# Expert stage with the weights stationary, token blocks of 448 rows and pad rows written beforehand

## The chip, the cores and the metric

The kernel runs on one core of one Trainium2 chip. Its time is the device time of one execution, in microseconds (us). The kernel before took 530.7 us, the median of three runs (530.37 to 531.23).

## The reference, cut to what matters

Cross attention and then a mixture of experts, in float32, on 16 sequences of 100 tokens with 256 features (1,600 tokens).

```python
x = x + xattn(layernorm(x), ctx, ctx, ...)   # 16 heads of 16, rope, window of the last 65 keys
h = layernorm(x)                             # 1600 x 256
probs = softmax(h @ router_w.T)              # 8 experts
topk_p, topk_i = top_k(probs, 2); topk_p /= topk_p.sum(-1)
for e in range(8):
    mask = (topk_i == e).any(-1)
    mean_w = w_tok.sum() / max(mask.sum(), 1)      # w_tok: the weights of e, one number per expert results
    eo = (silu(h @ gate_w[e].T) * (h @ up_w[e].T)) @ down_w[e].T    # 256 -> 1024 -> 256
    out += mask[:, None] * eo * mean_w
x = x + out
```

A token needs only its two chosen experts: 3,200 rows of work over eight experts.

## The kernel before

Attention stage (0 to about 200 us). The sequences go in eight pairs, in software pipeline. Loops over pair i and slot n (0 to 7) are written out in line, and each engine (`@block.tensor`, `scalar`, `vector`, `gpsimd`, `sync`) has its own order of work in them; semaphores are the only link. SyncE (SP) loads context and x in three parts (`load_rows`, L343): pair 0, pair 1, and, behind the key copies of pair 0, all the rest (L372). `key_blocks` (L354) copies the rotated keys of a pair into a block layout by 16 small transfers. ScalarE (ACT) loads the weights of expert 0 in slot 1 of pair 1 (L742). VectorE (DVE) asks for the third part of x in slot 7 of pair 0 (`xn_stats(2)`, L1037, L862), before the first maximum of pair 1. GpSimd (POOL) splits the weights of expert 0 and scatters each pair's normalized rows, with the row's number behind its 256 features, to the DRAM table `slots`, which has one region per expert (`scatter`, L1181).

Hand-over. DVE counts the tokens of each expert and makes from them the plan: the first and last tile of each expert, in one word that every engine loads (`tiles_of`, L241). POOL fills the rows behind each expert's last token with a pad row that points to spare output rows (L1222, eight indirect writes); SP waits for these and for the scatters before it loads tiles (L384 to L394).

Expert stage. A step is a tile of 128 rows of one expert. Matmuls run on float32r values that are split into a rounded high part and a remainder, and three products (high x high, high x low, low x high) make one. The token tile, transposed to features by tokens, is the stationary operand, and 512 weight columns move (`hidden`, L620; `three_products`, L611); this gives tokens by hidden features, which are transposed back in 128 x 128 pieces (`hidden_transpose`, L628) for the down projection (`project_down`, L635). ACT applies silu and rounds the high parts, DVE multiplies gate and up and takes the remainders. POOL scales the output by the expert's mean weight and adds it to `out` by an accumulating indirect write (L1245, L1250). The weights of expert e+1 are split on ACT and DVE during the first three steps of expert e, in twelve pieces of 512 columns, from one of two raw buffers. A loop over four pairs of experts holds two loops over tiles; the routing of these inputs gives 30 steps.

## Time and profile before

| | before |
|---|---|
| median of the runs | 530.7 us |
| fastest run | 530.37 us |
| span of the profiled execution | 528.9 us |
| TensorE busy | 476.4 us, 90% |
| VectorE, ScalarE, GpSimd busy | 321.5, 265.6, 186.4 us |
| attention stage, hand-over | 0 to 200 us, 200 to 224.7 us |
| expert stage, first to last matmul | 224.7 to 516.1 us |
| data moved | 46.26 MB |

The span is that of one profiled execution, from its first to its last instruction; for that execution no other time is given, and it is set beside the runs' median. The page gives the busy time of each engine, the span in 40 slices (13.2 us each) and the costliest groups of instructions. In the span's order, TensorE is nearly full in the attention stage, nearly empty in the hand-over and full again in the expert stage. In a row, the mean length of one matmul is longer than the distance between two, since matmuls overlap in the array; the distance is read from the starts.

### The profile page before, as it was taken

The numbers are of one execution on the slowest core, as the hardware profiler recorded it, in microseconds if no ns is written. First come the engines' busy times: TensorE is split into PE (matmuls) and PEld (weight loads), VectorE is DVE, ScalarE is ACT, GpSimd is POOL, SyncE is SP. The second block draws the span as 40 slices with busy tenths as digits, with TensorE's granted clock in tenths as the row PEclk, the third lists the DMA queues.
The fourth block names the chain that finished last, engine by engine and source line by source line (L and its number), as shares of the span: only waits on it lengthen the run. The fifth ranks groups of instructions, "written<-read, shape, count | busy, mean of one in ns | idle before, by whom it ended". The sixth has DMA issues, their size and how long they took to land. (4 is left out here: it accounts for less than half of the span.)

```text
span 528.9 us, 10721 instructions
## 1 busy us (share of the span) xinstructions
PE 476.4 (90%) x2879; PEld 375.3 (71%) x2880; DVE 321.5 (61%) x827; ACT 265.6 (50%) x878; POOL 186.4 (35%) x211
## 2 busy tenths in 40 slices
PE   2999999999999983199999999999999999999980
PEld 2656666665666542078888888888888888888870
DVE  3476988989998656345665456655655555553430
ACT  1287777677777870044544445544444444532320
POOL 5201327355372434712332323323333232232232
PEclk9699999999999995579999999999999999999996
DMA  7166102112020171371531634415317212112110
GB/s 210 33 184 241 32 12 54 32 34 63 7 58 14 50 286 47 96 274 32 168 117 35 215 83 139 147 32 196 101 20 256 42 20 32 27 21 39 20 20 10
DMA packets 21738, 46.26 MB, mean 87 GB/s; under 512 B 5032, under 2 KB 18600, under 8 KB 20684
## 3 DMA queue, kind: packets, MB, share of 16 engines
q10 hardware_dynamic: 1982, 23.29, 11.6%
q1 hardware_dynamic: 12974, 14.34, 9.3%
q0 software_dynamic: 6752, 8.29, 9.2%
q8 instruction: 11, 0.18, 0.1%
q14 instruction: 19, 0.16, 0.1%
HBM read 34.21 MB, written 10.04 MB: 84 GB/s over the span
## 5 line engine op out<-in xcount | busy, mean ns | idle before, releaser
L752 ACT ACTIVATE probs<-b_s,negmax 100x100 f32<-100x100 f32 x256 | 85.6, 358 | 25.2 <-DVE negmax L1005 21.8
L615 PE MATMUL b_s<-w_hi,x_hi 128*128 128x512 f32 x180 | 77.1, 428 | 1.1 <-issue 1.1
L617 PE MATMUL b_s<-w_hi,x_lo 128*128 128x512 f32 x180 | 72.3, 402 | 0.0
L616 PE MATMUL b_s<-w_lo,x_hi 128*128 128x512 f32 x180 | 72.2, 401 | 0.0
L640 PE MATMUL b_pv<-w_hi,h_hi 128*128 128x256 f32 x240 | 69.8, 291 | 1.4 <-DVE h_lo L1102 1.4
L640 PE MATMUL b_pv<-w_hi,h_lo 128*128 128x256 f32 x240 | 67.4, 281 | 0.0
L640 PE MATMUL b_pv<-w_lo,h_hi 128*128 128x256 f32 x240 | 67.3, 280 | 0.0
L1245 POOL TENSOR_SCALAR y_sb<-y_raw,mean 128x256 f32<-128x256 f32 x30 | 32.8, 1093 | 75.9 <-DVE y_raw L1109 75.7
L1250 POOL DMA_INDIRECT out<-y_sb,idnow x30 | 49.1, 1638 | 25.6 <-issue 23.0
L780 ACT CAST h_hi<-b_small 128x512 fp32r<-128x512 f32 x30 | 17.6, 587 | 80.7 <-PE b_small L631 80.7
L1116 DVE TENSOR_TENSOR w_lo<-w_raw,w_hi x84 | 57.3, 682 | 0.0
L752 ACT ACTIVATION_READ_ACCUMULATOR probs<-b_s,negmax 100x1 f32 x256 | 55.9, 218 | 0.0
L421 PE MATMUL b_s<-kblk,qrot 128*100 128x400 f32 x128 | 54.3, 505 | 0.0
L1102 DVE TENSOR_TENSOR h_lo<-b_small,h_hi 128x512 fp32r<-128x512 f32 x30 | 20.8, 692 | 55.0 <-ACT h_hi L780 55.0
L787 ACT CAST w_hi<-w_raw x84 | 52.2, 621 | 0.0
L776 ACT ACTIVATE act<-b_s 128x512 f32<-128x512 f32 x60 | 36.0, 600 | 28.6 <-PE b_s L617 28.6
L640 PEld LDWEIGHTS b_pv<-w_hi,h_hi 128*128 128x128 f32 x240 | 45.2, 188 | 3.0 <-DVE h_lo L1102 1.6
L640 PEld LDWEIGHTS b_pv<-w_lo,h_hi 128*128 128x128 f32 x240 | 45.3, 189 | 1.4
L640 PEld LDWEIGHTS b_pv<-w_hi,h_lo 128*128 128x128 f32 x240 | 45.2, 188 | 0.0
L1005 DVE TENSOR_REDUCE negmax<-b_s 100x4 f32<-100x400 f32 x64 | 36.2, 565 | 14.8 <-PE b_s L421 14.2
L1097 DVE TENSOR_TENSOR h_sb<-b_s,act 128x512 f32<-128x512 f32 x30 | 20.8, 692 | 34.7 <-PE b_s L617 34.7
L1176 POOL TENSOR_SCALAR ve<-mv 100x2 f32<-100x2 f32 x16 | 3.6, 228 | 103.8 <-DVE mv L859 103.8
(142 smaller groups left out, 1004.1 us busy)
## 6 DMA issues: line engine op xcount, KB each, us to landing
w_raw<-in_ffw ACTq DMA_DIRECT2D x7, 3072.0 KB, 10.1
xin<-slots SPq DMA_DIRECT2D x30, 128.5 KB
w_raw<-in_ffw SPq DMA_DIRECT2D x1, 3072.0 KB, 10.8
kblk<-krot SPq DMA_DIRECT2D x128, 12.5 KB, 1.8
out<-x_all SPq DMA_DIRECT2D x8, 200.0 KB
ctx_all<-in_ctxT SPq DMA_DIRECT2D x1, 1200.0 KB, 6.1
x_all<-in_x SPq DMA_DIRECT2D x1, 1200.0 KB
cst<-in_consts SPq DMA_DIRECT2D x1, 539.0 KB, 7.5
```

Of the source, the lines that this page charges most:

```text
L421: pe.matmul(o, qrot[:, i % 2, 2 * c + b, :], kblk[:, i % 2, c, h:h + QH, b * S:(b + 1) * S], start=False, stop=True).then_inc(s_s, 1)
L615: pe.matmul(o, lh, rh, start=(k == 0), stop=False)
L616: pe.matmul(o, lh, rl, start=False, stop=False)
L617: m = pe.matmul(o, ll, rh, start=False, stop=(k == n - 1))
L640: m = pe.matmul(b_y[:, 0:D], left[:, f, :], right[:, f, :], start=(f == 0 and k == 0), stop=(f == FC - 1 and k == 2))
L752: m = nc.scalar.activation(probs[:, N % 3, h, :], b_s[N % 3][0:S, h * S:(h + 1) * S], ACT.Exp, bias=negmax[:, N % 4, h:h + 1], accum_out=p ...
L776: nc.scalar.activation(act[:, half, :], b_gate[half][:, :], ACT.Silu).then_inc(s_act, 1)
L787: nc.scalar.copy(w_hi[1 - par][:, bass.ds(col, WC)], w_raw[par][:, bass.ds(col, WC)]).then_inc(s_whi, 1)
L1005: V.tensor_reduce(negmax[:, N % 4, :], b_s[N % 3][0:S, 0:QH * S].rearrange("p (h s) -> p h s", h=QH), AX.X, ALU.max, negate=True).then_inc ...
L1116: V.tensor_tensor(w_lo[1 - par][:, bass.ds(col, WC)], w_raw[par][:, bass.ds(col, WC)], w_hi[1 - par][:, bass.ds(col, WC)], ALU.subtract).t ...
L1245: G.tensor_scalar(y_sb[:, :], y_raw[:, :], mean1[:, 0:1], None, ALU.mult).then_inc(s_scaled, 1)
L1250: G.indirect_dma_start(out, bass.IndirectOffsetOnAxis(idnow[:, 0:1], 0), y_sb[:, :], None, bounds_check=TOK + P - 1, oob_is_err=True, comp ...
```

## The change

A block is now 448 rows of one expert: 4 groups of 112. A partition of the loaded block `xin` holds four successive rows of the table. The weights are the stationary operand, 128 hidden features at a time (chunk f, 0 to 7), and 448 tokens move; the result has hidden features on partitions and goes to the down projection without a transpose, where the hidden values are stationary and 256 weight columns move. Four row groups collect in two PSUM banks. ACT scales and evicts the output; POOL issues four accumulating writes per block. The experts are written out one after the other on each engine. The first block of an expert, in line, carries the splitting of the next expert's weights, in six pieces of 1,024 columns (half of a gate, up or down matrix), from one raw buffer that is refilled piece by piece; further blocks would run in a loop that the plan skips where an expert has one block.

The eight tail writes and the counts for them are gone. Instead ACT's queue writes pad rows over the whole table, in four transfers from a host array `padrows` in slot 1 of pairs 0, 2, 3 and 5, and each scatter waits for the parts that it can reach. The store of pad output rows covers 448 rows, comes from `padrows` and no longer waits for a memset. SP's register loads for expert 0 stand ahead of its wait for the scatters.

The diff, cut; conversions of x and of hidden values on ACT and DVE go by halves and chunks in the same way.

```diff
-TILE = 128
+GRP = 4
+ROWS = 112
+TILE = GRP * ROWS
 MAXT = -(-TOK // TILE)
-REGION = MAXT * TILE + TILE
+REGION = MAXT * TILE
...
-WC = 512
+WC = WT // 2
+WCH = 6
+FILLS = (0, 2, 3, 5)
...
+    pads = np.zeros((TILE, RW), np.float32)
+    pads[:, D:] = (TOK + np.arange(TILE, dtype=np.int32))[:, None].view(np.float32)
...
-            sp.wait_ge(s_zero, 2)
-            sp.dma_start(out[TOK:TOK + P, :], tailrow[:, 0:D]).then_inc(s_pad, 16)
+            sp.dma_start(out[TOK:TOK + TILE, :], padrows[:, 0:D]).then_inc(s_pad, 16)
...
-            sp.dma_start(w_raw[0][:, :], ffw[1]).then_inc(s_raw[0], 16)
+            for k in range(WCH):
+                sp.dma_start(w_raw[:, k * WC:(k + 1) * WC], ffw[1][:, k * WC:(k + 1) * WC]).then_inc(s_raw[k], 16)
...
-                sp.wait_ge(s_tails[e], 16)
+                if e == 0:
+                    for q in s_scat:
+                        sp.wait_ge(q, 16 * TOPK * 2 * (NPAIR // 2))
...
-                    sp.dma_start(xin[:, :], slots[bass.ds(row, TILE), :]).then_inc(s_in, 16)
+                    sp.dma_start(xin[:, :, :].rearrange("p g w -> p (g w)"),
+                                 slots[bass.ds(row, TILE), :].rearrange("(p g) w -> p (g w)", g=GRP)
+                                 ).then_inc(s_in, 16)
...
+            def hidden(par, t, f):
+                cols = slice(f * P, (f + 1) * P)
+                for which, banks, done in ((0, b_gate, s_gate), (1, b_up, s_up)):
+                    wh, wl = wpart(w_hi[par])[which], wpart(w_lo[par])[which]
+                    o = banks[f % 2][:, 0:TILE]
+                    for c in range(DC):
+                        if f == 0 and which == 0:
+                            pe.wait_ge(s_xlo, DC * t + c + 1)
+                        pe.matmul(o, wh[:, c, cols], x_hi[:, c, :], start=(c == 0), stop=False)
+                        pe.matmul(o, wh[:, c, cols], x_lo[:, c, :], start=False, stop=False)
+                        m = pe.matmul(o, wl[:, c, cols], x_hi[:, c, :], start=False, stop=(c == DC - 1))
+                    m.then_inc(done, 1)
+            def project_down(par, t, f):
+                pe.wait_ge(s_hlo, FC * t + f + 1)
+                if f == 0:
+                    pe.wait_ge(s_y, t + 1)
...
+                for g in range(GRP):
+                    o = b_y[g // 2][0:ROWS, g % 2 * D:(g % 2 + 1) * D]
+                    for k, (left, right) in enumerate(((h_hi, wh), (h_hi, wl), (h_lo, wh))):
+                        m = pe.matmul(o, left[:, f, g * ROWS:(g + 1) * ROWS], right[:, f, :],
...
+            def step(t, par, next_par, next_split, last):
+                for f in range(1, FC):
+                    if f >= 2:
+                        pe.wait_ge(s_h, FC * t + f - 1)
+                    if f == FC - 1 and not last:
+                        pe.wait_ge(s_xlo, DC * t + DC)
+                        tile_transpose(t + 1)
+                    hidden(par, t, f)
+                    if f >= 2:
+                        project_down(par, t, f - 2)
+                project_down(par, t, FC - 2)
+                if not last:
+                    pe.wait_ge(s_wlo, next_split)
+                    hidden(next_par, t + 1, 0)
+                project_down(par, t, FC - 1)
...
+            for e in range(E):
+                par = e % 2
+                lo, hi, end = tiles_of(pe, e)
+                with pe.If(end - lo), pe.Fori(lo, end) as t:
+                    step(t, par, par, WCH * (e + 1), False)
+                step(end, par, 1 - par, WCH * (e + 2), e == E - 1)
...
+            def fill_pads(j):
+                a.dma_start(slots.rearrange("(e j p g) w -> j e p (g w)", j=MAXT, p=ROWS, g=GRP)[j],
+                            padrows.rearrange("(p g) w -> p (g w)", g=GRP).unsqueeze(0)
+                            .to_broadcast([E, ROWS, GRP * RW])).then_inc(s_pre[j], 16)
...
+                    if n == 1 and i in FILLS:
+                        fill_pads(FILLS.index(i))
...
+            def take_output(t, e):
+                a.wait_ge(s_down, t + 1)
+                a.wait_ge(s_idnow, t + 1)
+                a.wait_ge(s_mean, 1)
+                for n in range(GRP // 2):
+                    m = nc.scalar.activation(y_sb[:, 2 * n:2 * n + 2, :].rearrange("p g d -> p (g d)"),
+                                             b_y[n][0:ROWS, :], ACT.Copy, scale=meanw[0:ROWS, e:e + 1])
+                m.then_inc(s_y, 1)
+            def step(t, e, par, split, again, final=False):
+                for f in range(FC):
+                    if f:
+                        if f == FC - 1 and not final:
+                            a.wait_ge(s_up, FC * (t + 1))
+                            x_high(t + 1)
+                        silu(t, f)
+                    hidden_high(t, f)
+                    if split and f < WCH:
+                        weights_high(e, par, f)
+                    if split and again and 1 <= f <= WCH:
+                        reload(e, f - 1)
                 if not final:
                     silu(t + 1, 0)
+                take_output(t, e)
...
+                for j in range(MAXT):
+                    if j * TILE < (i + 1) * PT:
+                        g.wait_ge(s_pre[j], 16)
...
+                for n in range(GRP):
+                    G.indirect_dma_start(out, bass.IndirectOffsetOnAxis(idnow[:, n:n + 1], 0), y_sb[:, n, :], None,
```

## Rows read from the trace of the kernel before

**Rows 1.** The page: TensorE's share, and its clock in 40 slices.

```profile
PE 476.4 (90%) x2879; PEld 375.3 (71%) x2880; DVE 321.5 (61%) x827; ACT 265.6 (50%) x878; POOL 186.4 (35%) x211
...
PEclk9699999999999995579999999999999999999996
```

**Rows 2.** TensorE's waits, 230.9 to 516.1 us: total, times, longest.

```profile
PE b_pv L640 <- DVE h_lo L1102: 1.4, 1, 1.4
```

**Rows 3.** Stretches: PE, PEld, DVE, ACT, POOL busy us (count), clock, DMA share, GB/s.

```profile
224.70:230.70 6.00, 5.46 (x12) 3.82 (x12) 0.49 (x1) 1.24 (x2) 2.02 (x4) 0.50 0.50 132
230.90:516.10 285.20, 283.71 (x1726) 249.93 (x1726) 154.08 (x292) 124.83 (x232) 86.89 (x93) 1.00 0.33 92
```

**Rows 4.** TensorE in order of time: start, length, line, shape.

```profile
383.71 0.60 PE L631 MATMUL b_small<-cst,h_sb 128*128 128x128 f32 x4
384.07 0.48 PE L615 MATMUL b_s<-w_hi,x_hi 128*128 128x512 f32 x1
384.38 0.40 PE L616 MATMUL b_s<-w_lo,x_hi 128*128 128x512 f32 x1
...
386.73 0.39 PE L617 MATMUL b_pt<-w_hi,x_lo 128*128 128x512 f32 x1
...
387.30 0.28 PE L640 MATMUL b_pv<-w_lo,h_hi 128*128 128x256 f32 x1
...
388.47 0.28 PE L640 MATMUL b_pv<-w_hi,h_lo 128*128 128x256 f32 x1
```

**Rows 5.** Groups of conversions: count, busy us, mean ns.

```profile
L1116 DVE TENSOR_TENSOR w_lo<-w_raw,w_hi x84 | 57.3, 682 | 0.0
...
L787 ACT CAST w_hi<-w_raw x84 | 52.2, 621 | 0.0
```

**Rows 6.** SP's waits over the span.

```profile
SPq L385 <- DMA slots<-xrow,desti: 16.2, 1, 16.2
```

**Rows 7.** Order of time, 201 to 225 us, SP, POOL and TensorE.

```profile
201.43 0.29 SPq L367 DMA_DIRECT2D out<-x_all  x1
...
213.92 0.99 POOL L1186 DMA_INDIRECT slots<-xrow,desti  x1 [0.30 <-issue]
...
215.22 0.99 POOL L1186 DMA_INDIRECT slots<-xrow,desti  x1 [0.30 <-issue]
...
221.20 0.00 SPq L394 DMA_DIRECT2D xin<-slots  x1
...
222.91 0.66 PE L608 MATMUL b_proj<-cst,xin 128*128 128x128 f32 x2 [6.27 <-DMA xin<-slots]
...
224.71 0.77 PE L615 MATMUL b_s<-w_hi,x_hi 128*128 128x512 f32 x1 [1.14 <-issue]
```

**Rows 8.** Four stretches, columns as in rows 3.

```profile
28.00:36.00 8.00, 7.57 (x51) 4.58 (x50) 6.05 (x14) 7.04 (x36) 0.00 (x0) 1.00 0.75 201
36.00:38.00 2.00, 2.00 (x10) 1.42 (x9) 1.45 (x4) 1.84 (x10) 0.00 (x0) 1.00 0.23 58
38.00:40.00 2.00, 1.64 (x12) 0.82 (x10) 1.62 (x4) 1.27 (x7) 0.00 (x0) 1.00 0.08 20
46.00:50.00 4.00, 4.00 (x26) 3.20 (x25) 3.17 (x8) 3.14 (x14) 0.00 (x0) 1.00 1.00 430
```

**Rows 9.** DMA queues from 9 to 10 us: packets, MB, share.

```profile
q10 hardware_dynamic: 86, 0.21, 75.4%
q1 hardware_dynamic: 90, 0.07, 26.8%
```

**Rows 10.** SP's transfers in order of time, 20 to 64 us.

```profile
23.70 0.61 SPq L344 DMA_DIRECT2D ctx_all<-in_ctxT  x1
24.35 0.54 SPq L345 DMA_DIRECT2D x_all<-in_x  x1
```

**Rows 11.** DVE at the end of pair 0.

```profile
39.47 0.74 DVE L855 BATCH_NORM_STATS2 stats<-x_all 100x6 f32<-100x256 f32 x2
```

**Rows 12.** The last write of the kernel.

```profile
518.55 1.60 POOL L1250 DMA_INDIRECT out<-y_sb,idnow  x1 [0.84 <-issue]
```

More of the change, by code:

```diff
@@ L61 @@
 C_BASE = C_EXP + E
-C_TAIL = C_BASE + E
-C_THR = C_TAIL + E
+C_THR = C_BASE + E
 C_LT = C_THR + E * (MAXT - 1)
@@ L317, in build @@
         s_in = sem("s_in")
-        s_xt = sem("s_xt")
+        s_xt = [sem(f"s_xt{c}") for c in range(DC)]
         s_xhi = sem("s_xhi")
@@ L637, in project_down @@
+                    m.then_inc(done, 1)
[3 more added lines that the diff above has]
+                    pe.wait_ge(s_y, t + 1)
                 wh, wl = wpart(w_hi[par])[2], wpart(w_lo[par])[2]
-                for f in range(half * HF, (half + 1) * HF):
+                for g in range(GRP):
+                    o = b_y[g // 2][0:ROWS, g % 2 * D:(g % 2 + 1) * D]
                     for k, (left, right) in enumerate(((h_hi, wh), (h_hi, wl), (h_lo, wh))):
-                        m = pe.matmul(b_y[:, 0:D], left[:, f, :], right[:, f, :],
-                                      start=(f == 0 and k == 0), stop=(f == FC - 1 and k == 2))
@@ L783, in weights_high @@
[L783 to L800 removed]
+                for c in range(DC):
+                    a.wait_ge(s_xt[c], t + 1 + c)
+                    nc.scalar.copy(x_hi[:, c, :], b_xt[c][:, 0:TILE]).then_inc(s_xhi, 1)
@@ new lines, in step, with expert, last_expert @@
+                take_output(t, e)
+            def expert(e, par, again):
+                lo, hi, end = tiles_of(a, e)
+                step(lo, e, par, True, again)
+                with a.If(end - lo), a.Fori(lo + 1, hi) as t:
+                    step(t, e, par, False, False)
+            def last_expert(e, par):
+                lo, hi, end = tiles_of(a, e)
+                with a.If(end - lo), a.Fori(lo, end) as t:
+                    step(t, e, par, False, False)
+                step(end, e, par, False, False, final=True)
@@ L828, in _ @@
             x_high(0)
             silu(0, 0)
-            with a.Fori(0, E // 2 - 1) as ep:
-                for par in range(2):
-                    expert(2 * ep + par, par, a.to_reg(16 * (ep + 2 - par)), True)
-            expert(E - 2, 0, 16 * (E // 2 + 1), False)
-            expert(E - 1, 1, None, False)
+            for e in range(E - 1):
+                expert(e, e % 2, e + 2 < E)
+            last_expert(E - 1, 1)
         @block.vector
@@ L1091, in take_ids @@
+            def take_ids(t):
                 v.wait_ge(s_in, 16 * (t + 1))
[L1092 to L1103 removed]
@@ new lines, in step @@
+            def step(t, e, par, split, final=False):
+                for f in range(FC):
+                    if f:
+                        if f == FC - 1 and not final:
+                            x_low(t + 1)
+                        gated(t, f)
+                    hidden_low(t, f)
+                    if split and f < WCH:
+                        weights_low(e, par, f)
+                    if f == FC - 2 and not final:
+                        v.wait_ge(s_idnow, t + 1)
+                        take_ids(t + 1)
@@ L1134, in step, with expert @@
                 if not final:
                     gated(t + 1, 0)
[L1137 to L1152 removed]
+            def expert(e, par):
+                lo, hi, end = tiles_of(v, e)
+                step(lo, e, par, True)
+                with v.If(end - lo), v.Fori(lo + 1, hi) as t:
+                    step(t, e, par, False)
@@ L1154, in _, with last_expert @@
+            def last_expert(e, par):
+                lo, hi, end = tiles_of(v, e)
+                with v.If(end - lo), v.Fori(lo, end) as t:
+                    step(t, e, par, False)
+                step(end, e, par, False, final=True)
             x_low(0)
-            take_ids(0, slice(0, 1))
+            take_ids(0)
             gated(0, 0)
-            with v.Fori(0, E // 2 - 1) as ep:
-                for par in range(2):
-                    expert(2 * ep + par, par, True)
-            expert(E - 2, 0, True)
@@ L1161, in _ @@
-            expert(E - 1, 1, False)
+            for e in range(E - 1):
+                expert(e, e % 2)
+            last_expert(E - 1, 1)
         @block.gpsimd
```

342 lines of the change are left out of this document (90 added, 252 removed).

## The prediction

> **What bounds the kernel now.** I read the page's busy shares and clock row first, then the waits of the expert stage, then stretches of it, and last the order of single instructions. TensorE is busy 90% of the span; its granted clock falls to the lower level (1.2 GHz) twice, in the second slice (13 to 26 us) and from 200 us until the expert stage is under way [rows 1]. In the expert stage TensorE's longest wait in 285 us is 1.4 us [rows 2], and it is busy 283.7 of 285.2 us at the upper level [rows 3]. So that stage is worth what TensorE's instructions cost, and nothing else. The attention stage (0 to 200 us) is a fixed order on five engines with about 3 us of slack between neighbours; what enters it late is paid in full.
>
> How the pieces are priced [rows 4]: ten 512-column matmuls start in 2.35 us, 0.235 each; ten 256-column ones in 1.17 us, 0.117 each; four transposes take 0.36 us and delay the matmul behind them by 0.08, 0.11 each. A step of today is 24 x 0.235 + 24 x 0.117 + 10 x 0.11 = 9.55 us; 30 of them, less the 2.8 us of matmuls that the last one lacks, make 283.7 us, which is the busy time of [rows 3].
>
> **The change, part by part.**
>
> Number of blocks. Today's 30 steps are 128-row tiles. The inputs' routing gives the experts 374, 410, 299, 390, 438, 418, 425 and 446 tokens (the reference's top-2 choice, counted). All are under 448, so there are 8 blocks, one per expert, and no loop over blocks ever runs a second time.
>
> TensorE. Hidden: 8 blocks x 8 chunks x 2 (gate, up) x 2 x 3 = 768 matmuls of 448 columns, at 0.235 x 448/512 = 0.206: 157.9 us (today 720 x 0.235 = 169.2). Down: 8 x 8 x 4 row groups x 3 = 768 of 256 columns at 0.117: 89.9 us (today 84.2; it grows, since 112 of 128 output rows are used). Transposes of the hidden values (240) vanish, since the hidden values now come out with features on partitions; those of tokens are 8 a block, 56 behind the first, 6.9 us with the delays. The first 6 us run at the lower clock as today [rows 3]: 3.2 us more. Waits 0.5. Sum 258.4, against 516.1 - 224.7 = 291.4: **-33.0 us**. Nine tenths of it are the transposes; in columns the two kernels nearly tie. Bounds: a 448-column matmul from 0.187 (columns at the ideal share of 2.4 GHz) to 0.235, -47 to -10; I take the proportional value, because 256 and 512 columns are proportional within 1%.
>
> Does ACT and DVE work keep up? A chunk is 12 x 0.206 + 12 x 0.117 = 3.88 us of TensorE. A converted 512-column piece costs 0.62 on ACT and 0.68 on DVE [rows 5]. Per chunk a chain runs: product on DVE (at most 0.68), its rounding on ACT (0.62), weight piece of 1,024 columns on ACT (at most 1.24), its remainder on DVE (at most 1.36), then the next product: 3.9, with two hops of 0.1 at most 4.1, and 3.7 if fixed cost is shared. Six such chunks fall behind by at most 1.3 us; the hidden matmuls of chunk f need only the product of f-2, which leaves 1.4 us. So 0. If it is late the cost is (chain - 3.88) x 6 x 7: 0 to +15. The token conversion between blocks (after the last hidden matmul: 0.62 and 0.68 for the first half, plus hops, 1.5) lies under two down chunks (2.8). The output pass on ACT (1.2) lies under two hidden chunks (4.9). The six 512 KB reloads have a whole block (32 us) to land; today 3 MB needs a third of that. Queued behind ACT's output pass is the rounding of the next block's first chunk, needed 4.9 us later.
>
> Hand-over. Today SP waits 16.2 us from the end of its last store issue (201.7) for the scatters, to 217.9, then issues the first token load at 221.2 [rows 6, 7]; it has landed at 222.9, and the first hidden matmul starts at 224.7 [rows 7]. The eight tail writes, of which SP waits for one, and SP's two register loads leave that stretch; address work stays. Load issued at 218.9 (bounds 218.2 to 221.2). It carries 460 KB instead of 132: 329 KB more at 430 GB/s [rows 8], 0.8 us, so 221.4. Four transposes at the lower clock (0.7), one conversion each on ACT and DVE (0.6, 0.7) and hops (0.4): start at 223.8, **-0.9** (-2 to +2). DVE's shorter plan lies under SP's wait: 0. GpSimd's weight pieces are the same elements: 0.
>
> End. Today TensorE ends at 516.1 and the one accumulating write is issued from 518.55 for 1.60 us [rows 12]. Now ACT's two passes replace copy and scaling (-0.3), and four writes are issued in place of one. Scatters of 0.99 us follow each other in 1.30 [rows 7], so 1.9 each for three more: +5.7 (4.8 with no gap, 7.3 with the widest). **+5.4**. In other blocks these 8 us lie under 32.
>
> Start. The pad store is 448 rows instead of 128, and from DRAM, in front of the first key copies, which have 7 us: +0.3 (0 to 1.4).
>
> Pad rows. This part decides. ACT's queue sends four writes of 8 x 448 x 1,028 B = 3.68 MB each, the first in pair 0, slot 1, near 24 us. That is when SP issues the last token loads: 1.2 MB context at 23.70 and 1.2 MB x at 24.35 [rows 10]. The 128-row weight load keeps all 16 DMA engines full at 430 GB/s, 27 each; the x load (100 rows) shows a share of 0.75 against 0.08 with key copies alone, some 10 engines [rows 8]: the outer count shared evenly. The fill's outer count is 8, so 8 engines, 460 KB each, 17.1 us. Two queues on the same engines take turns by packets: 86 to 90 in the microsecond where both are full [rows 9]. The x load has more packets per engine (120, plus 16 of context) than the fill (112 of 4,112 B), so the whole fill goes in between. The x load ended near 36.45 (the share of 0.23 in 36 to 38 us is 0.08 and 0.45 us of the load's 0.67); now it ends at 53.6. DVE asks for it at 39.47, in slot 7 of pair 0 [rows 11], and the scores of pair 1 need key copies queued behind it: a stall of **+14.5 us** for all engines. TensorE then idles, and its clock goes low as it did at 200 us [rows 1]; it came back 6 us after work began at 224.7 [rows 3]. Half of some 7 us: **+3.5** (0 to 5). The later fills (pairs 2, 3, 5) meet only key copies, each of which waits for one packet of 0.15 us and has 3 us: 0.
>
> By the Trainium skill, "DMA: Bandwidth & Descriptors" (Why a DMA increments its semaphore by 16 and not by 1), a transfer uses the largest count up to 16 that divides its slowest dimension: 8 here, and 10 for the x load, where the trace agrees (about 10.6 by the shares); with 16 engines the stall would be as in rival B.
>
> **Sum.** -33.0 - 0.9 + 5.4 + 0.3 = -28.2 without the stall, +18.0 with it: -10.2. The profiled span is 528.9 us and the runs' median 530.7, so 1.8 us lie around it; they stay. 530.7 - 10.2 = **520.5 us**.
>
> **Rivals.**
> B: the fill runs on all 16 engines, or the x load gets a better share. Then it is late by 8.6, the stall is 6.0 and the clock costs 2: 510.5. For it: nothing shows an outer count of 8.
> C: no collision, because ACT's fill is generated slowly or late and x is through first: 502.5. Against it: the two are issued within a microsecond and queues share evenly.
> D, slower: a fill packet, read from DRAM and written to DRAM, pays both ways in turn, 0.30 us instead of 0.15. The x load is then 33.6 us late, the stall 31, the clock 3.5: 537. It turns the sign once a packet costs over 0.244 us (27.3 us / 112). For it: no DRAM-to-DRAM row exists here; against: reads at 27 GB/s per engine already include a write.
> E: code in line. Each of seven expert changes makes TensorE jump over an unused block body of some 400 instructions. Today's loop-backs cost nothing (1.5 us idle in 285 [rows 3]), yet those are backward. At up to 2 us each, +14: 534.5 with the collision. The late conversion chain would look alike in size.
> Against this part speaks the Trainium skill, "Runtime: NRT & Kernel Launch" (Instruction fetch mechanics): prefetch is sequential and a taken branch out of the window waits for a fetch. No run here shows a forward jump of this length; by that rule the time is E's, by the loop rows it is the forecast.
>
> **How the numbers follow.** Forecast 0.45 (own range 512 to 530), B 0.15, C 0.20, D 0.12, E 0.08. Differences under 0.2% (1 us) can't be told from none. Faster: 0.41 + 0.15 + 0.20 + 0.02 = 0.78; within 0.2%: 0.03; slower: 0.12 + 0.05 + 0.02 = 0.19. Range 502 to 538: half of C's and D's outer sides are left out.
>
> **What would show it.** TensorE idle from about 41 to 54 us with DVE's statistics of pair 2 waiting for x; granted clock 0.5 behind it; the fill's queue busy from 24 to 52 us at half the engines. 768 hidden starts 0.206 apart, 768 down starts 0.117 apart, blocks 32 us apart without gaps at f = 4 to 6 or at the expert changes. Four accumulating issues 1.9 us apart at the end. Wrong if x lands by 39 us, if blocks are over 33 us apart, or if the last matmul is later than 502 us.

## The result: slower, 557.9 against 531.0 us

| | before | after | forecast |
|---|---|---|---|
| median of the runs | 530.97 (530.37 to 531.70) | 557.93 (550.69 to 558.38) | 520.5 (502 to 538) |
| ratio to before | | 1.047 [1.041, 1.053] | 0.981 |
| span of the profiled execution | 528.9 | 556.5 | 518.7 |
| first to last scores of the attention stage | 20.39 to 190.32 | 22.08 to 229.11 | 20.7 to 208.6 |
| its pair 0 | 19.1 | 35.2 | 37.1 |
| its pairs 1 to 6 together | 134.6 | 155.6 | 134.6 |
| last scores to first hidden matmul | 34.4 | 35.1 | 33.5 |
| expert stage, first hidden to last down | 291.4 | 275.5 | 258.4 |
| from there to the end | 12.9 | 16.8 | 18.3 |

A pair is measured from the first scores matmul of one pair to that of the next. The median is 37.4 us above the forecast. Against the forecast the profiled execution lost 1.4 at the start, won 1.9 in pair 0, lost 21.0 in pairs 1 to 6, 1.6 in the hand-over and 17.1 in the expert stage, and won 1.5 at the end: 37.7 in sum. Of the 21.0, pair 1 has 2.8: until 63.1 us TensorE ran it at the lower clock, behind the stall of pair 0. The 1.4 at the start is no effect of the change: in the profiles below the first scores start anywhere from 19.5 to 22.0 us, with the same work in front of them.

The page after, as [rows 1]: TensorE's share, and its clock in 40 slices of 13.9 us.

```profile
PE 462.6 (83%) x2739; PEld 374.8 (67%) x2739; DVE 302.0 (54%) x716; ACT 266.4 (48%) x845; POOL 138.1 (25%) x130
...
PEclk9759799889999899955799998999999899999995
```

Before, the granted clock fell twice, at the start and in the hand-over. Now it also falls between 28 and 70 us, around 110, 140 and 190 us, and three times for 3.4 us in the expert stage (at 271, 340 and 442 us); the shortest falls hardly show in slices of 13.9 us. Each stands behind a stretch in which TensorE was short of work.

**Pair 0.** The first rows are TensorE's waits from 20 to 60 us: total, times, longest ("issue" is idle time that nothing in the profile ends). Behind them stand the transfers that ACT issues, then those of SP from 20 us and from 60 us, each with its start and the time that its issue took. The last two rows are the DMA queues from 36 to 38 us: packets, MB and share of the 16 engines.

```profile
PE b_s L406 <- DMA kblk<-krot: 12.8, 2, 12.3
PE b_s L406 <- issue: 3.3, 1, 3.3
```

```profile
23.90 0.82 ACTq L701 DMA_DIRECT2D slots<-in_padrows  x1
```

```profile
19.56 6.32 SPq L345 DMA_DIRECT2D kblk<-krot  x10
25.92 0.66 SPq L329 DMA_DIRECT2D ctx_all<-in_ctxT  x1
26.62 0.70 SPq L330 DMA_DIRECT2D x_all<-in_x  x1
```

```profile
71.30 11.43 SPq L345 DMA_DIRECT2D kblk<-krot  x16
...
122.79 14.46 SPq L345 DMA_DIRECT2D kblk<-krot  x16
```

```profile
q10 hardware_dynamic: 8, 0.46, 53.2%
q1 hardware_dynamic: 90, 0.08, 11.8%
```

ACT issues the pad write at 23.90. SP issued its loads at 23.70 and 24.35 before [rows 10]; now it has the key copies of pair 0 in hand until 25.9, and the loads follow at 25.92 and 26.62, behind the write. The last two rows show what the prediction had wrong. The write (q10) moves 0.46 MB in 8 packets, so a packet has 57,568 bytes, not 4,112, and takes 2.1 us (8 x 2.1 us are 53% of the 32 us that 16 engines have in 2 us). Each packet is fourteen rows of 4,112 bytes, which are contiguous in source and destination. A key copy behind such a packet waits 2.1 us instead of 0.15. The SP rows show it: the 16 copies of pair 4 take 14.46 us to issue, those of pair 2, with no write beside them, 11.43. DVE's statistics of pair 2, which the prediction had as the victim of the write, start here, with a wait of only 1.25 us:

```profile
55.62 0.75 DVE L840 BATCH_NORM_STATS2 stats<-x_all 100x6 f32<-100x256 f32 x2 [1.25 <-DMA x_all<-in_x]
```

**Hand-over,** as [rows 7]: SP's token load, the transposes, the first hidden matmul.

```profile
258.20 0.37 SPq L379 DMA_DIRECT2D xin<-slots  x1
```

```profile
261.70 0.98 PE L596 MATMUL b_proj<-cst,xin 112*128 112x112 f32 x4 [6.80 <-DMA xin<-slots]
...
264.18 0.71 PE L609 MATMUL b_s<-x_hi,w_hi 128*128 128x448 f32 x1 [0.75 <-DVE x_lo L1065]
```

**Expert stage.** TensorE's waits over it, as [rows 2]; two stretches, as [rows 3]; and TensorE in order of time where expert 2's (the third expert's) loop over further blocks is skipped, in front of chunk 1 of its only block:

```profile
PE b_s L609 <- issue: 13.2, 6, 2.7
PE b_s L609 <- DVE x_lo L1065: 0.8, 1, 0.8
```

```profile
270.90:539.70 268.80, 257.92 (x1580) 241.84 (x1580) 136.26 (x189) 121.65 (x195) 46.45 (x35) 0.98 0.38 94
339.30:343.30 4.00, 4.00 (x12) 3.58 (x13) 1.29 (x2) 0.90 (x2) 3.39 (x3) 0.57 0.37 38
```

```profile
339.25 0.48 PE L609 MATMUL b_s<-x_hi,w_hi 128*128 128x448 f32 x1 [2.35 <-issue]
339.56 0.55 PE L610 MATMUL b_s<-x_lo,w_hi 128*128 128x448 f32 x1
339.90 0.57 PE L611 MATMUL b_s<-x_hi,w_lo 128*128 128x448 f32 x1
...
343.14 0.37 PE L611 MATMUL b_pt<-x_hi,w_lo 128*128 128x448 f32 x1
343.35 0.37 PE L609 MATMUL b_s<-x_hi,w_hi 128*128 128x448 f32 x1
```

The wait is put down to "issue": nothing that the profile shows releases the first hidden matmul behind the skipped loop. Each of the eight experts has such a loop (the prediction counted seven changes); there are six gaps, at 271.28, 339.25, 374.98, 441.17, 476.62 and 510.81, 13.2 us in all, and none near 305 and 407 us. Behind the gap of 2.35 us hidden matmuls start 0.37 apart instead of 0.21 until 343 us: the granted clock of these 4 us is 0.57, and the same happens behind the gaps of 2.73 and 2.20 us. A block takes some 34 us (275.5 us for eight), where the prediction had 32. Elsewhere hidden starts are 0.206 apart and down starts 0.118, as forecast.

**End,** as [rows 12]: four writes, 1.77 us apart (forecast 1.9).

```profile
541.84 1.48 POOL L1193 DMA_INDIRECT out<-y_sb,idnow  x1 [20.97 <-ACT y_sb L782]
543.62 1.46 POOL L1193 DMA_INDIRECT out<-y_sb,idnow  x1 [0.30 <-issue]
545.39 1.46 POOL L1193 DMA_INDIRECT out<-y_sb,idnow  x1 [0.30 <-issue]
547.15 1.46 POOL L1193 DMA_INDIRECT out<-y_sb,idnow  x1 [0.30 <-issue]
```

### The profile page after: what moved, and what is told of

Same layout as the page of the kernel before. It is cut to its first block, busy times and chain, and to the rows that moved or that the text cites. A ratio compares the mean times of both kernels' runs of the same rounds, so it can differ in the third digit from the quotient of the medians.

```text
span 556.5 us, 8741 instructions
## 1 busy us (share of the span) xinstructions
PE 462.6 (83%) x2739; PEld 374.8 (67%) x2739; DVE 302.0 (54%) x716; ACT 266.4 (48%) x845; POOL 138.1 (25%) x130
## 4 chain that ended last, share of the span: by engine, by line
PE 66%; issue 10%; DVE 7%; ACT 7%; DMA 5%; POOL 2%; SPq 2%; ACTq 0%; POOLq 0%; DVEq 0%
PE b_small L622 8%; PE b_o L622 8%; PE b_s L609 8%; PE b_s L610 7%; PE b_s L611 7%; PE b_s L408 5%; ACT probs L736 4%; PE b_pv L431 3%; PE b_pt L609 3%; PE b_pt L611 2%; PE b_pt L610 2%; DMA kblk<-krot 2%; PE b_pt L417 2%; PE b_o L506 2%; PE b_s L406 2%
## 5 line engine op out<-in xcount | busy, mean ns | idle before, releaser
L609 PE MATMUL b_s<-x_hi,w_hi 128*128 128x448 f32 x192 | 73.6, 383 | 14.0 <-issue 13.2
L765 ACT CAST h_hi<-h_sb 128x448 fp32r<-128x448 f32 x64 | 36.3, 567 | 78.1 <-DVE h_sb L1075 77.0
L610 PE MATMUL b_s<-x_lo,w_hi 128*128 128x448 f32 x192 | 72.2, 376 | 0.0
L611 PE MATMUL b_s<-x_hi,w_lo 128*128 128x448 f32 x192 | 72.1, 376 | 0.0
L1079 DVE TENSOR_TENSOR h_lo<-h_sb,h_hi 128x448 fp32r<-128x448 f32 x64 | 40.1, 627 | 55.6 <-ACT h_hi L765 55.0
L1084 DVE TENSOR_TENSOR w_lo<-w_raw,w_hi 128x1024 fp32r<-128x1024 f32 x42 | 51.5, 1226 | 13.7 <-ACT w_hi L770 13.7
L609 PEld LDWEIGHTS b_s<-x_hi,w_hi 128*128 128x128 f32 x192 | 37.1, 193 | 18.3 <-issue 15.7
L406 PE MATMUL b_s<-mask_bf,ident_bf 100*100 100x400 bf16 x64 | 24.4, 381 | 26.5 <-issue 13.7
L770 ACT CAST w_hi<-w_raw 128x1024 fp32r<-128x1024 f32 x42 | 44.0, 1047 | 0.0
L611 PEld LDWEIGHTS b_s<-x_hi,w_lo 128*128 128x128 f32 x192 | 37.2, 194 | 3.4
L1134 POOL TENSOR_SCALAR ve<-mv 100x2 f32<-100x2 f32 x16 | 3.6, 224 | 143.7 <-DVE mv L844 143.7
L610 PEld LDWEIGHTS b_s<-x_lo,w_hi 128*128 128x128 f32 x192 | 37.4, 195 | 2.5
L1147 POOL DMA_INDIRECT slots<-xrow,desti x32 | 34.5, 1079 | 15.8 <-DVE desti L968 8.3
```

Source lines behind the costliest of these rows:

```text
L406: pe.matmul(o, ident_bf[0:S, 0:S], mask_bf[0:S].rearrange("p h s -> p (h s)"), start=True, stop=False)
L609: pe.matmul(o, wh[:, c, cols], x_hi[:, c, :], start=(c == 0), stop=False)
L610: pe.matmul(o, wh[:, c, cols], x_lo[:, c, :], start=False, stop=False)
L611: m = pe.matmul(o, wl[:, c, cols], x_hi[:, c, :], start=False, stop=(c == DC - 1))
L770: nc.scalar.copy(w_hi[1 - par][:, cols], w_raw[:, cols]).then_inc(s_whi, 1)
L1079: V.tensor_tensor(h_lo[:, f, :], h_sb[:, f % 2, :], h_hi[:, f, :], ALU.subtract).then_inc(s_hlo, 1)
```

## The experiments

All times are medians. The ratio is to the kernel before, with its 95% interval. Pair 0, pairs 1 to 6 and the expert stage are measured as above, in one profiled execution each. The combinations are listed behind the single edits. The changed kernel and the five variants that leave the expert stage alone took 272.8 to 276.5 us in it, so a difference of 2 us there decides nothing.

| kernel | time | ratio [95%] | pair 0 | pairs 1-6 | expert stage |
|---|---|---|---|---|---|
| before | 531.0 | | 19.1 | 134.6 | 291.4 |
| changed | 557.9 | 1.047 [1.041, 1.053] | 35.2 | 155.6 | 275.5 |
| fill16 | 537.4 | 1.010 [1.007, 1.013] | 28.6 | 142.1 | 276.5 |
| fill8small | 599.0 | 1.127 [1.125, 1.130] | 40.7 | 192.8 | 274.6 |
| fill0only | 545.3 | 1.029 [1.026, 1.032] | 36.7 | 142.1 | 272.8 |
| fill8mid | 544.3 | 1.024 [1.021, 1.026] | 34.5 | 145.0 | 274.3 |
| nobody | 538.6 | 1.013 [1.009, 1.016] | 35.3 | 158.2 | 256.7 |
| tinybody | 538.9 | 1.014 [1.011, 1.018] | 36.0 | 155.8 | 256.1 |
| lag4 | 550.2 | 1.036 [1.033, 1.040] | 36.1 | 154.3 | 268.3 |
| pool512 | 556.0 | 1.046 [1.044, 1.048] | 35.6 | 155.1 | 275.0 |
| combo | 519.2 | 0.979 [0.973, 0.984] | 18.9 | 138.6 | 269.4 |
| latefill | 520.3 | 0.979 [0.976, 0.982] | 18.6 | 141.6 | 269.6 |
| combo1024 | 526.5 | 0.992 [0.990, 0.994] | 19.3 | 143.7 | 271.1 |
| comboone | 504.6 | 0.951 [0.948, 0.954] | 18.9 | 136.3 | 258.0 |

### The pad writes

**fill16**: partitions outermost instead of experts, for all four writes. This gives 16 engines and keeps rows of 4,112 bytes apart.

```diff
-slots.rearrange("(e j p g) w -> j e p (g w)", ...)[j], padrows....unsqueeze(0).to_broadcast([E, ROWS, GRP * RW])
+slots.rearrange("(e j p g) w -> j p e (g w)", ...)[j], padrows....unsqueeze(1).to_broadcast([ROWS, E, GRP * RW])
```

> The four pad fills with the partition dimension outermost (112 outer, the experts inner), so that a fill runs on 16 DMA engines in packets of 4,112 B in place of 8 engines and 57,568 B; same bytes, same slots. Theory P (a queue that shares an engine with the fill gets one packet per fill packet of 2.1 us, so key copies of pairs 0, 3, 4 and 6 and the last token load come late): the later fills (5.3, 6.8 and 3.8 us in pairs 2, 3 and 5) cost under 1 us each; in pair 0 the key copies wait for packets of 0.16 us and only the x load is late, by the fill's 9 us, so 4 to 7 us are left of 16. Together 22 to 30 us faster than the changed kernel: 528 to 536. Rival Q (what counts is that 14.7 MB stand in front of the small transfers, whatever their packets): the same bytes on 16 engines hold them half as long but hit all of them; 0 to 8 us faster.

**fill8small**: experts outermost, but four writes, one for each row of a group of four, so that a packet has 1,028 bytes (the scatters wait for all four).

```diff
+for g in range(GRP):
+    a.dma_start(slots.rearrange("(e j p g) w -> j g e p w", ...)[j, g], padrows....[g].unsqueeze(0).to_broadcast([E, ROWS, RW]))
```

> Each fill as four transfers, one per row of a partition's group of four, the experts outermost: still 8 engines, same bytes, packets of 1,028 B in place of 57,568. Theory P: the packet's length is what costs, so the key copies are on time again in all pairs; the x load of pair 2 alternates with fill packets of 0.05 us and is late by 17 us or a little less, so pair 0 keeps 10 to 14 of its 16 us; pairs 2, 3 and 5 lose theirs (16 us). Total 12 to 20 us faster than the changed kernel: 538 to 546. Rival Q: no change within 3 us. If small packets are slow in themselves (over 0.1 us each), the fills take over 45 us and the later scatters, which wait for them, become late: slower than the changed kernel.

**fill0only**: the first write alone; scatters wait for it only, and pad rows behind the first 448 rows of a region are left unwritten.

```diff
-if n == 1 and i in FILLS:
+if n == 1 and i == FILLS[0]:
```

> Only the first fill (first block of each expert, pair 0) is sent; the other three, which cover rows that no expert reaches with these inputs, are left out, and scatters wait for the first alone. Theory P: pair 0 keeps its 16 us, pairs 2, 3 and 5 return to the lengths of the kernel before: 14 to 18 us faster than the changed kernel, 540 to 544. Rival R (the long stall in pair 0 and the clock behind it shift everything, the later fills cost nothing): under 4 us faster.

fill16 took 20.5 us off, just short of the 22 to 30 expected. Its pair 2 takes 23.9 us and its pairs 3 to 6 take 24.4, exactly as in fill0only, which has no later writes: in this form they cost nothing. In pair 0 it keeps 9.5 of the 16.1 us, more than the 4 to 7 expected: TensorE still waits for key copies, although the packets are short. The write is still ahead of the loads, and its packets take 95% of all engines' time from 26 to 30 us; that this is the reason was not tested.

```profile
PE b_s L406 <- DMA kblk<-krot: 8.5, 2, 8.1
```

fill0only shows the later writes' share in the changed kernel: pairs 1 to 6 fall from 155.6 to 142.1, 13.5 us. Not all of that is the later writes. Pair 1 falls from 23.4 to 20.7, and it ends before the second write is issued (80.7 and 85.1 us). What differs there is the granted clock: its mean over pair 1 is 0.88 in the changed kernel and 1.00 in fill0only. It is 1.00, and pair 1 20.6, in pool512 as well, which has all writes as in the changed kernel. The later writes' own share is that of pairs 2 to 6: from 132.2 to 121.5, 10.8 us. Its time fell by 12.6 us, somewhat less than the 14 to 18 expected, since its pairs 2 to 6 did not return to their old lengths but stay 1.5 us longer each; "GpSimd's pieces" below has the reason.

fill8small did not behave as its main expectation had it: pairs 0, 2, 3 and 5 take 40 to 42 us each. The DMA engines are not the reason, since each write is through 27 to 35 us behind its first packet. ACT's queue shows where the time went, in pair 0 (with ACT's next instruction) and in pair 2:

```profile
25.63 21.21 ACTq L702 DMA_DIRECT2D slots<-in_padrows  x2
46.88 0.34 ACT L737 ACTIVATE probs<-b_s,negmax 100x100 f32<-100x100 f32 x1 [21.96 <-issue]
```

```profile
87.51 16.74 ACTq L702 DMA_DIRECT2D slots<-in_padrows  x4
```

Issuing the third and fourth of the four writes held ACT for 21.2 us in pair 0 and for 13.6 to 15.1 us in each of the three later pairs, and ACT could not compute in that time; in the changed kernel the issue of a whole write takes 0.7 to 0.8 us. So fill8small doesn't test the length of the packets: it exchanged that cost for another one, ACT's. Its key copies of pair 0 were late by 8.1 us all the same.

The form that the prediction had priced was still untried: eight engines, 4,112 bytes. **fill8mid** has it, in two writes of every second row, which can't be joined (the scatters wait for both).

```diff
+dst = slots.rearrange("(e j q r g) w -> j r e q (g w)", j=MAXT, r=2, q=ROWS // 2, g=GRP)
+src = padrows.rearrange("(q r g) w -> r q (g w)", r=2, g=GRP)
+for r in range(2):
+    a.dma_start(dst[j, r], src[r].unsqueeze(0).to_broadcast([E, ROWS // 2, GRP * RW])).then_inc(s_pre[j], 16)
```

> The changed kernel, with each pad write given as two of every second row, so that rows of 4,112 bytes can't be merged into packets of 57,568; the outer count is still 8. This is the write that the prediction priced (8 engines, 4,112 B). Theory M (what the prediction missed is the merged packet, in front of which every key copy waits 2.1 us): the write takes about 17-20 us, the token load still ends near 53, pair 0 is 32-35 us, the later pairs with writes come down to 24.4-25.5 as with 16 engines: last scores near 217-220, time 543-548. Rival H (eight engines are enough to stop the key copies, whatever the packet): pairs 2, 3 and 5 stay at 27-30 us, 555-558. If the packets turn out slower in themselves, as those of 1,028 B did, worse than 558.

The queues of fill8mid from 36 to 38 us, and the stall that the prediction described, where it described it (DVE on x, then TensorE):

```profile
q10 hardware_dynamic: 81, 0.33, 40.5%
q1 hardware_dynamic: 136, 0.13, 18.8%
```

```profile
54.63 0.75 DVE L842 BATCH_NORM_STATS2 stats<-x_all 100x6 f32<-100x256 f32 x2 [7.98 <-DMA x_all<-in_x]
```

```profile
56.28 0.54 PE L406 MATMUL b_s<-mask_bf,ident_bf 100*100 100x400 bf16 x1 [10.03 <-issue]
```

81 packets share the 2 us with 136 of SP's, where the changed kernel had 8 and 90. Statistics of pair 2 start at 54.63, behind a wait of 8.0 for x; the forecast was 39.47 + 14.5 = 54.0. Pair 0 is 34.5, and the pairs with later writes are 23.9 to 24.4. Pairs 2 to 6 take 121.4 us, as without later writes; pair 1 takes 23.6, at a mean clock of 0.87. The time fell by 13.7 us, inside the range that theory M gave, and ACT's issues take 0.7 to 0.8 us each as before; eight engines alone do not stop the key copies. In pair 0 they are still late, by 4.5 us. By the Trainium skill, "DMA: Bandwidth & Descriptors" (Queues, rings and completion order), an engine drains a whole packet of one queue before it turns to the next; the trace agrees, with turns of 2.1 us in the one kernel and 0.16 in the other.

### The expert changes

**nobody** leaves TensorE's loop over further blocks out (no expert may then have more than 448 tokens); **tinybody** keeps branch and loop, but cuts its body from some 400 instructions of TensorE to the 12 matmuls of one chunk and their weight loads (its result for a second block would be incomplete).

```diff
 with pe.If(end - lo), pe.Fori(lo, end) as t:      # nobody: both lines gone
-    step(t, par, par, WCH * (e + 1), False)
+    hidden(par, t, 1)                             # tinybody
```

> TensorE's loop over further blocks of an expert is left out (no expert has one with these inputs), so TensorE has no unused body of about 400 instructions to jump over at the eight experts; nothing else changes. Theory E (a jump over the body waits for instructions): the seven gaps of 1.8 to 2.7 us before the first hidden matmul behind an expert's change vanish, and with them the three falls of the clock: 14 to 20 us faster than the changed kernel, 538 to 544. Rival F (the gap is the register load of the plan word, or a wait for ACT or DVE that the profile doesn't name): the gaps stay, within 2 us.

> TensorE's loop over further blocks keeps its branch and its loop, but its body holds only one hidden chunk (12 matmuls) instead of 200; it is never run with these inputs, so nothing computed changes. Theory E1 (the length jumped over is what costs, since the instructions behind it have not been fetched): no gap at the expert changes, as without the body, 538 to 541. Rival E2 (the branch and the loop set-up cost the gap themselves): gaps of 1.8 to 2.7 us stay, 555 to 558.

A stretch of the stage in nobody, and one in tinybody, columns as [rows 3]:

```profile
271.00:521.40 250.40, 250.40 (x1575) 236.61 (x1573) 135.21 (x190) 120.37 (x196) 45.09 (x35) 1.00 0.40 100
```

```profile
271.00:519.00 248.00, 248.00 (x1563) 234.31 (x1562) 133.49 (x189) 118.95 (x194) 45.36 (x35) 1.00 0.40 101
```

TensorE is busy in all of both, at the upper clock, and both stages take 256 to 257 us; both times are in the expected range. So neither branch nor loop costs anything here; the length of the code that is jumped over does, 19 us over eight loops, of which 13.2 are the gaps and some 5 the clock behind three of them (3.4 us at half rate each). What TensorE waits for in a gap no row names; that it is the supply of instructions is inferred.

**lag4** keeps the bodies and moves work: down runs four chunks behind hidden instead of two, and the next expert's first hidden chunk comes last.

```diff
-if f >= 2: project_down(par, t, f - 2)
+if f >= 4: project_down(par, t, f - 4)
...
+for f in range(FC - 4, FC): project_down(par, t, f)
 if not last:
     pe.wait_ge(s_wlo, next_split)
     hidden(next_par, t + 1, 0)
-project_down(par, t, FC - 1)
```

> TensorE's down projections run four chunks behind the hidden ones in place of two, and the first hidden chunk of the next block comes last in a block; bodies and branches stay. Theory E (the jump over the body takes about 5 us of instruction supply, of which the matmuls already queued hide 2.9; with the hidden chunk last the queue holds about 4.8): gaps at the expert changes shrink from 2.2 to under 0.7 us and the clock no longer falls there, 10 to 18 us faster than the changed kernel, 540 to 548. Rival F2 (the sequencer stalls before it has queued the block's last matmuls, so that order changes nothing): gaps of 2 us stay, 555 to 560. If the lag of four makes a product or an output late, waits for DVE or ACT appear inside the blocks.

```profile
PE b_s L609 <- issue: 10.2, 7, 1.7
```

This missed its expectation (540 to 548 us, gaps under 0.7). Seven gaps are left, of 1.5 us on average. The clock stays up behind all of them: the stage is 7.2 us shorter, which is the clock's 5 and a part of the gaps. The clock's part is not certain with this order: latefill and combo1024 below have it too, and there it fell once each, behind gaps of 1.84 and 2.21 us. No run moved the code of the further blocks out of the way while keeping it, so the full 19 us have only been recovered by a kernel that assumes one block per expert.

### GpSimd's pieces

**pool512**: each of GpSimd's six pieces of 1,024 columns in two halves again.

```diff
+for half in range(2):
+    cols = slice((i - 1) * WC + half * WC // 2, (i - 1) * WC + (half + 1) * WC // 2)
     G.tensor_copy(w_hi[0][:, cols], w_raw[:, cols])
     G.tensor_tensor(w_lo[0][:, cols], w_raw[:, cols], w_hi[0][:, cols], ALU.subtract)
```

> GpSimd converts expert 0's weights in pieces of 512 columns again, two in a row per pair, in place of one of 1,024; nothing else changes. Theory G (DVE's second normalizing instruction can't run while GpSimd's long subtraction does, and waits for its end: 3.5 us for the two instructions against 2.0 before and 0.7 alone): the 1.2 to 1.5 us that each of pairs 2 to 6 is longer vanish, 6 to 9 us faster than the changed kernel, 549 to 552; DVE's normalizing pair takes 2.0 us. Rival H (the longer pairs come from the order of GpSimd's work after the first stall, not from the length of its pieces): no change within 2 us.

Alone it gave 1.9 us, less than the changed kernel's own runs differ, and nothing to speak of in the attention stage (155.1 against 155.6): a miss. In the changed kernel few normalizations meet a piece of GpSimd: the median of the 16 instructions is 0.41 us, against 1.12 in fill16. The length of DVE's normalization `xn` (ns: least, median, greatest), before and in fill16, shows the term where nothing covers it:

```profile
L871 DVE TENSOR_SCALAR xn<-x_all,mv,rstd x16: 405/682/1430, 10.4 to 155.2; 100x256 f32<-100x256 f32 x16
```

```profile
L856 DVE TENSOR_SCALAR xn<-x_all,mv,rstd x16: 408/1116/2512, 11.5 to 172.5; 100x256 f32<-100x256 f32 x16
```

To settle it, the three mends were put together and one taken out again.

**combo** is fill16, with the first write in slot 6 of pair 0 (`n == (1 if i else 6)`), pool512 and lag4. **combo1024** is combo without pool512.

> Together: fills on 16 engines in packets of 4,112 B, the first one in slot 6 of pair 0 in place of slot 1, GpSimd's pieces of 512 columns, and the down projections four chunks behind. If the costs add: from 558 the attention stage gives back 36 to 38 us (16 us stall, its clock, 14 us of later fills, 9 us of long GpSimd pieces) and the expert stage 10 to 18: 503 to 513, faster than the kernel before by 18 to 27 us. If the x load is still late because the fill meets its end (slot 6 is at 34 to 37 us), 2 to 6 us more. If a lone cause had been behind several of the losses, it stays above 515.

> The combination, with GpSimd's weight pieces in one part of 1,024 columns again (6 pieces, pairs 1 to 6). Theory G (the normalization on DVE waits for the whole GpSimd instruction, and the attention order has no slack for it): six pairs of 24.4 us instead of 22.9, +9 us: 527-529. The longest normalization grows from 1.43 to 2.5 us. Rival N (the 1.5 us a pair that the later pad writes cost is what made 24.4): pairs stay at 22.9, 519-520.

GpSimd, DVE and TensorE in order of time, in combo1024 and then in combo, each with TensorE's costliest wait from 50 to 200 us behind it:

```profile
114.92 1.03 POOL L1170 CAST w_hi<-w_raw 128x1024 fp32r<-128x1024 f32 x1
...
114.99 3.54 DVE L856 TENSOR_SCALAR xn<-x_all,mv,rstd 100x256 f32<-100x256 f32 x2 [0.69 <-POOL rstd L1137]
...
116.03 2.35 POOL L1173 TENSOR_TENSOR w_lo<-w_raw,w_hi 128x1024 fp32r<-128x1024 f32 x1
...
118.58 0.56 PE L445 MATMUL b_small<-cst,xn 100*128 100x100 f32 x4 [1.17 <-DVE xn L856]
```

```profile
PE b_small L445 <- DVE xn L856: 5.0, 5, 1.2
```

```profile
112.31 0.60 POOL L1171 CAST w_hi<-w_raw 128x512 fp32r<-128x512 f32 x1
...
112.37 2.04 DVE L856 TENSOR_SCALAR xn<-x_all,mv,rstd 100x256 f32<-100x256 f32 x2 [0.56 <-POOL rstd L1137]
...
112.99 1.27 POOL L1174 TENSOR_TENSOR w_lo<-w_raw,w_hi 128x512 fp32r<-128x512 f32 x1
```

```profile
PE b_pv L431 <- ACT probsT L719: 1.9, 5, 0.4
```

In combo1024 the normalization starts 0.07 us behind GpSimd's conversion and ends at 118.53, just behind the subtraction of 1,024 columns (116.03 + 2.35); TensorE waits 1.17 us for it. In combo it starts beside pieces of 512, lasts 2.04, and TensorE waits for it no more. The four steady pairs (3 to 6) are 22.88 us each, as before; in combo1024 24.38. That makes 6.0 us, and pair 2 adds 1.0; the time differs by 7.3. With 526.5 us combo1024 came out just under the 527 to 529 that theory G gave it. The same 1.5 us a pair are what fill0only and fill16 have more than before in pairs 2 to 6, 7.5 us in sum. The Trainium skill, "SBUF — State Buffer" (Who interferes with whom), says that a `tensor_scalar` of DVE in a two-port mode and GpSimd share a port pair that one holds for its whole instruction. The trace agrees: the same normalization of two instructions takes 0.73, 2.0 or 3.5 us by what GpSimd runs beside it; in which mode DVE ran, no row shows.

### What combo still pays

combo is faster than both kernels: 519.2 us, 1.6 to 2.7% under before. It missed its expectation of 503 to 513, because two costs are left: pair 1 takes 24.7 us (20.6 before), with the first write beside it, and the expert stage has seven gaps, 11.1 us. A part of pair 1 is the clock: its mean there is 0.93 in combo, but 1.00 in comboone, which has the same attention code and takes 22.3 us for the pair. So the write beside it costs 1.7 us, and a further 2.3 where the clock falls too. **latefill** moves the first write to pair 1, slot 4 (FILLS = (1, 2, 3, 5)); **comboone** leaves out the loops over further blocks, as nobody does.

> The combination, with its first pad write moved from pair 0, slot 6 (issued near 38 us) to pair 1, slot 4 (near 52 us, behind the first expert's 3 MB of weights on the same queue). In the combination pair 1 takes 24.7 us against 20.6 before, with 3.6 us of waits for key copies. Theory P (a fill beside the end of the token load and the 3 MB load is what pair 1 pays for): pair 1 returns to 20.6-21.5, last scores at 190-191.5 instead of 193.9, time 515-518 against 519.2. Rival S (the first scatters now wait for the later fill): pair 2 or 3 grows by what pair 1 gives back, 519-521.

> The combination, with TensorE's loops over further blocks left out (this kernel can't handle an expert of more than 448 tokens). Theory J (what is left at the seven expert changes is the jump over some 400 instructions): the seven gaps of 1.3-1.8 us go, 12 us: 506-508, expert stage 257 us instead of 269. Rival C (with the down step four chunks behind, the gaps are the conversion chain or a weight reload that comes late): the gaps stay with another wait named, 517-519.

latefill missed the 515 to 518 of theory P. Pair 1 still takes 25.5 us, with an idle TensorE for the last 4.4 of them, and pair 2 now 24.7 (22.45 in combo), since the clock is at the lower level for its first 4.6 us. The time is the one that rival S gave, but not by its mechanism, since GpSimd's waits in front of its scatters are the same as in combo (5.8 us for DVE's `desti` in both) and none is for a pad write. Where the write would cost nothing is open. Two stretches of the expert stage, combo and comboone, and comboone's clock row:

```profile
235.00:498.00 263.00, 253.30 (x1578) 237.21 (x1579) 135.46 (x190) 120.28 (x196) 49.61 (x35) 1.00 0.38 96
```

```profile
233.00:484.00 251.00, 250.77 (x1566) 234.81 (x1565) 134.63 (x190) 119.21 (x196) 44.48 (x35) 1.00 0.40 100
```

```profile
PEclk9899999999999999558999999999999999999995
```

comboone's stage is 258.0 us, the forecast's 258.4, and its time 504.6, a little under the expected 506 to 508: 14.6 under combo, of which 11.4 in the stage and 2.3 in pair 1, by the clock.

## Why the prediction was wrong, step by step

The part that "decides", in its words, came close to its price. The sum was wrong by three terms that it had set to nothing: the later pad writes (10.8 us by fill0only), GpSimd's longer pieces (7.5, what pairs 2 to 6 of fill0only still have over before) and the skipped loops (17.1 over the forecast's expert stage). Together they are 35.4 of the 37.7 us that the profiled execution was late; start, pairs 0 and 1, hand-over and end make up the rest.

- **"The later fills (pairs 2, 3, 5) meet only key copies, each of which waits for one packet of 0.15 us and has 3 us: 0."** Failed, and the largest miss in the attention stage: packets were 2.1 us. Pairs 2 to 6 are 10.8 us shorter with 4,112 bytes (fill8mid), just as much as without later writes (fill0only). The packet size had been taken from the inner row of the source; that successive rows are contiguous on both sides, so that they can be joined, was in the diff.
- **"GpSimd's weight pieces are the same elements: 0."** Failed: the elements are the same, but one instruction twice as long holds DVE up, 1.5 us in each steady pair (combo1024 against combo). The trace of before had the sign: `xn` took 405 to 1,430 ns for one and the same shape.
- **Rival E, "code in line", chance 0.08.** This rival was right, and the sum had its cost at nothing. The loops over further blocks cost 19.4 us by the time (nobody), more than the 14 given, since three of the gaps also brought the clock down. The evidence used against it was that the backward jumps of the kernel before cost nothing; it does not carry over to long forward ones. The rule of the Trainium skill's "Runtime: NRT & Kernel Launch" (Instruction fetch mechanics) was right here and was given too little; the forward jump over a short body (tinybody) cost nothing, which fits it too.
- **Pad rows in pair 0, +14.5 and +3.5 of clock.** Close in size, but in the changed kernel not by the mechanism given, so that the near hit is in part luck. Pair 0 grew by 16.1 us and pair 1, with the lower clock in it, by 2.8: 18.9 against 18.0. The stall was to run from 41 to 54 us, with DVE waiting for x. Instead TensorE stood 12.3 us until 38.21, for the last key copies of pair 0, which were still on their way when the write came; the prediction had no term for them. DVE waited 1.25 us for x. In fill8mid, with the packets as priced, the mechanism shows as it was given (8.0 us of wait for x, TensorE idle for 10.0 behind it), next to 4.5 us for key copies; pair 0 grew by 15.4 and pair 1, again with the lower clock, by 3.0. Since key copies were late by 8.1 us with short packets too (fill16), the packet's length is only a part of what held them in pair 0; the rest is open.
- **TensorE in the expert stage, 258.4.** Right: 256.7 in nobody, 258.0 in comboone. The conversion chain kept up in both. **End, +5.4:** +3.9, since the writes are 1.77 apart instead of 1.9, and the end follows the start of the last write by 9.3 us instead of 10.4. **Hand-over, -0.9:** +0.7. The load was issued 29.1 us behind the last scores (30.9 before), but landed in 3.5 us instead of 2.5.
- **Rival B, 16 engines:** the write ran on eight (53% of 16 for 8 packets at a time), as forecast. fill16 makes it 16, and pair 0 then grew by 9.5 us, where B had 8.0. **Rival C, 502.5 without a collision,** is near what comboone measures, 504.6, with the other costs taken out too. **Rival D,** the dear packet, did not hold: in the forecast's form a packet takes 0.16 us (fill8mid), not 0.30, and under the 0.244 at which it would turn the sign.
- **Slips of under 1 us in the sum.** The transposes that vanish are 240 x 0.11 = 26.4 us, eight tenths of the 33.0 and not nine; the 56 token transposes are 6.2 us by the same price, not 6.9; and a conversion chain of 4.1 us is late by 9 us in all, not 15.

The terms don't add freely: in the changed kernel pool512 gives at most 2 us, and where the writes are harmless 7.3.

## What to carry to other kernels

A transfer that no engine waits for is priced by what shares its DMA engines: look at the length of its packets after adjacent rows are joined, not at the row in the source, and at where it falls against the loads of its neighbours. Look also at how long its issue holds the engine that issues it, above all when it is cut into many small rows. Making an instruction of GpSimd twice as long is not neutral when DVE works beside it in a schedule without slack. Code that is skipped at run time has a price where it is jumped over, if it is long: compare with a short body before trusting that an untaken loop is free.

## What the hardware showed that was not expected

- A DRAM to DRAM write of 8 x 112 rows of 4,112 bytes went out as 64 packets of 57,568 bytes, 2.1 us each; as rows of 4,112 bytes (fill8mid) a packet takes 0.16 us, nearly the same rate (27 and 26 KB per us and engine). In rows of 1,028 bytes, as four transfers, the same write took 27 to 35 us, and issuing the last two of them held ACT for 13.6 to 21.2 us (fill8small).
- A jump over some 400 instructions left TensorE without work for 1.3 to 2.7 us in nearly every case; over 24 instructions never.
- In the changed kernel the granted clock went to 0.5 for 3.4 us behind gaps of 2.73, 2.35 and 2.20 us, and stayed up behind 2.08, 2.06 and 1.79; behind lag4's gaps of 1.3 to 1.7 it always stayed up. The length of the gap alone does not decide it: in fill8mid the clock fell behind one of 2.01 us and stayed up behind one of 2.53.
- A normalization of 256 columns on DVE takes 0.41 us alone, up to 1.43 beside pieces of 512 columns on GpSimd and up to 2.51 beside pieces of 1,024 (before and fill16).
